# Down projection of a routed feed-forward as three products of rounded pieces, with the pieces streamed from DRAM

## What is computed

```python
xn = _rms_norm(x, scale)
ids = jnp.argmin(_dist2(xn, centroids), axis=-1)
for e in range(8):
    h = jnp.einsum('bsd,dh->bsh', xn, up_w[e])          # 256 -> 2*512
    a, g = jnp.split(h, 2, axis=-1)
    y = jnp.einsum('bsh,hd->bsd', a * silu(g), down_w[e])  # 512 -> 256
    out = jnp.where((ids == e)[..., None], y, out)
x = _layernorm(x + out + skip)
```

## Time and profile before

| | |
|---|---|
| median of 3 runs | 1208.92 us (1208.32 to 1210.83) |
| the profiled execution | 1210.72 us, span from first to last instruction 1209.0 us |
| TensorE / VectorE busy | 92% / 79% of the span |
| ScalarE / GpSimd busy | 55% / 64% |
| mean granted clock | 0.98 |
| data moved | 178.0 MB, 147 GB/s over the span |

### The profile page before, as it was taken

How to read it: one execution, slowest core, us unless ns; L and a number is a source line. 1 busy time by engine, 2 the same in 40 slices (tenths; PEclk the granted TensorE clock), 3 DMA queues, 4 the chain that set the end, 5 groups by cost and what they waited for, 6 DMA issues and landing times.

```text
span 1209.0 us, 27857 instructions
## 1 busy us (share of the span) xinstructions
PE 1114.7 (92%) x8283; PEld 831.4 (69%) x8315; DVE 957.7 (79%) x2437; ACT 667.6 (55%) x1417; POOL 771.6 (64%) x933
## 2 busy tenths in 40 slices
PE   4899998999999999999999999889999999999996
PEld 3766665666666666666666666668788888888885
DVE  7558998999999999999999998978755555555553
ACT  4266775777777776777777777663222222222221
POOL 4736888888998998998889884246433333333333
PEclk9989998999999999999999999979999999999998
DMA  5767777665665656656655645113554444454442
GB/s 127 188 166 203 179 193 173 199 161 148 153 152 153 154 138 155 159 150 152 158 136 157 149 118 132 39 30 103 174 159 137 148 153 154 153 153 146 147 153 88
DMA packets 124097, 178.04 MB, mean 147 GB/s; under 512 B 13670, under 2 KB 111599, under 8 KB 117776
## 3 DMA queue, kind: packets, MB, share of 16 engines
q1 hardware_dynamic: 117456, 159.65, 50.2%
q0 software_dynamic: 6528, 16.99, 4.7%
HBM read 124.47 MB, written 53.03 MB: 147 GB/s over the span
## 4 chain that ended last, share of the span: by engine, by line
PE 39%; DVE 36%; issue 10%; POOL 7%; DMA 4%; SPq 2%; ACT 1%; POOLq 0%; DVEq 0%; ACTq 0%
DVE neg_max_sb L1556 14%; PE Y L488 10%; PE G L450 8%; PE A L450 8%; DVE oq L1755 4%; DVE u L1574 4%; POOL buckets L849 3%; PE GT L460 2%; POOL state L805 2%; PE M L1186 2%; PE S L1229 2%; DMA neg_max<-nm_row 2%; DVE stx L1540 2%; PE O L1178 2%; DVE st L1540 1%
## 5 line engine op out<-in xcount | busy, mean ns | idle before, releaser
L1556 DVE TENSOR_REDUCE neg_max_sb<-S 128x2 f32<-128x512 f32 x512 | 327.5, 681 | 41.4 <-PE S L1229 40.8
L1019 ACT ACTIVATE probs<-T 128x512 f32<-128x512 f32 x512 | 277.7, 595 | 138.2 <-PE T L1242 123.8
L1229 PE MATMUL S<-k_st,q_st 48*128 48x256 f32 x1024 | 208.3, 312 | 33.0 <-DVE neg_max_sb L1556 30.9
L1229 PEld LDWEIGHTS S<-k_st,q_st 48*128 48x128 f32 x1024 | 141.3, 185 | 104.5 <-issue 71.5
L1242 PE MATMUL T<-q_st,k_st 49*128 49x256 f32 x1024 | 206.2, 313 | 6.8 <-ACT probs L1019 3.0
L1242 PEld LDWEIGHTS T<-q_st,k_st 49*128 49x128 f32 x1024 | 142.2, 187 | 22.0 <-ACT probs L1019 14.6
L428 ACT ACTIVATE gT<-GT 128x512 f32<-128x512 f32 x71 | 42.4, 598 | 207.1 <-PE GT L460 203.7
L1178 PE MATMUL O<-probs,v_aug 128*32 128x256 f32 x2048 | 141.4, 395 | 0.8 <-ACT probs L1019 0.7
L408 POOL DMA_INDIRECT out<-res,token x71 | 76.0, 1070 | 102.1 <-DVE res L575 97.0
L488 PE MATMUL Y<-dn_sb,gT 128*128 128x256 f32 x568 | 134.5, 379 | 2.4 <-DMA dn_sb<-in_L_ffn_down_w 1.7
L849 POOL DMA_INDIRECT buckets<-row,slot x64 | 68.9, 1077 | 82.9 <-DVE slot L1810 71.9
(11 more groups left out here) (210 smaller groups left out, 2599.0 us busy)
## 6 DMA issues: line engine op xcount, KB each, us to landing
dn_sb<-in_L_ffn_down_w SPq DMA_DIRECT2D x71, 512.0 KB
k_st<-k_pieces SPq DMA_DIRECT2D x64, 256.0 KB, 3.8
q_st<-q_pieces SPq DMA_DIRECT2D x64, 256.0 KB, 3.6
xr<-buckets SPq DMA_DIRECT2D x71, 129.0 KB
xt<-in_x SPq DMA_DIRECT2D x32, 256.0 KB, 6.2
ct<-in_ctx SPq DMA_DIRECT2D x32, 256.0 KB, 6.9
k_pieces<-k_hi SPq DMA_DIRECT2D x32, 256.0 KB, 3.6
k_pieces<-k_lo SPq DMA_DIRECT2D x32, 256.0 KB, 3.7
```

Of the source, the lines that this page charges most:

```text
L1019: a_.activation(probs[:, h % 8].rearrange("p k t -> p (k t)"), T_ps[h % 2][:, :], ACT.Exp, scale=DH ** -0.5).then_inc(s["exp_ok"], 1)
L1229: last = t_.matmul(S_ps[h % 2][:, c * TOK:(c + 1) * TOK], q_st[h // HPC][base:base + STACK, h % HPC, c * P:(c + 1) * P], k_st[h // HPC][ba ...
L1556: v.tensor_reduce(neg_max[:, cur.mod(2), :, h], S_ps[h % 2][:, :].rearrange("p (c t) -> p c t", c=NTC), AX.X, ALU.max, negate=True).then_i ...
```

## The change

The down projection is done as the up projection is: three float32r products (hi x hi, hi x lo, lo x hi) in place of one float32 product. For that `down_w` is cut once. Ahead of the attention steps SyncE loads all 4 MB of it into the still empty `up_sb`; in step 0 ScalarE rounds the 8 experts (`upper_down`), in steps 0 and 1 VectorE subtracts (`lower_down`), and in steps 1 to 8 SyncE stores both pieces of one expert each (2 x 512 KB) into the new DRAM tensor `down_pieces`. `UP_STEPS` moves to steps 9 to 16. In phase two a tile's `load_down` brings both pieces, 1 MB in rows of 8 KB, where it was 512 KB in rows of 1 KB. `gT` becomes a rounded piece from ScalarE, with a single buffer, and a rest from VectorE, and Y waits for the rest. `gated` takes the place of `gate` in SBUF, and some small tensors of phase two move.

```diff
@@ constants
-UP_STEPS = (0, 1, 2, 3, 4, 5, 6, 7)
+DOWN_STEPS = (1, 2, 3, 4, 5, 6, 7, 8)
+UP_STEPS = (9, 10, 11, 12, 13, 14, 15, 16)
+DOWN_HI_AT = {(0, h): (h // 2,) for h in range(0, H, 2)}
+DOWN_LO_AT = {(0, 5): (0,), (0, 8): (1,), (0, 11): (2,), (0, 14): (3,), (1, 2): (4,), (1, 6): (5,), (1, 10): (6,), (1, 14): (7,)}
@@ build()
+        down_dram = nc.dram_tensor("down_pieces", (E, P, 2 * DNW), F32)
@@ experts()
-            gT = sb2("gT", [P, 2, HCH * P])
-            dn_sb = sb2("dn_sb", [P, 2, DNW])
+            gated = gate
+            gT = sb2("gT", [P, 2, HCH * P], F32R)
+            dn_sb = sb2("dn_sb", [P, 2, 2, DNW], F32R)
...
-            dn_v = down_w.rearrange("e (o p) n -> p (e o) n", p=P)
+            dn_v = down_dram.rearrange("e p n -> p e n")
@@ experts(), load_down(d) on SyncE
-                    sp.dma_start(dn_sb[:, d.mod(2)].rearrange("p (o n) -> p o n", o=HCH), dn_v[:, bass.ds(r, HCH), :]).then_inc(dn_in[d.mod(2)], 16)
+                    sp.dma_start(dn_sb[:, d.mod(2)].bitcast(F32).rearrange("p (a w) n -> p a (w n)", a=1), dn_v[:, bass.ds(r, 1), :])\
+                        .then_inc(dn_in[d.mod(2)], 16)
@@ experts(), ScalarE
-                        wait(act, "y_pe", m - 2)
-                        a_.activation(gT[:, m.mod(2)], GT_ps[:, :], ACT.Copy).then_inc(z["gT_ok"], 1)
+                        wait(act, "y_pe", m - 1)
+                        a_.activation(gT[:, 0], GT_ps[:, :], ACT.Copy).then_inc(z["gT_ok"], 1)
@@ experts(), TensorE
-                        wait(pe, "gT_ok", m - 1)
+                        wait(pe, "gT_lo", m - 1)
...
-                        wait(pe, "gT_ok", m)
+                        wait(pe, "gT_lo", m)
                         wait(pe, "y2_ok", m - 1)
-                        for c in range(HCH):
-                            last = t_.matmul(Y_ps[:, 0:C], gT[:, m.mod(2), c * P:(c + 1) * P], dn_sb[:, m.mod(2), c * C:(c + 1) * C],
-                                             start=(c == 0), stop=(c == HCH - 1))
+                        terms = [(w, d, c) for c in range(HCH) for w, d in ((0, 0), (0, 1), (1, 0))]
+                        for k, (w, d, c) in enumerate(terms):
+                            last = t_.matmul(Y_ps[:, 0:C], gT[:, w, c * P:(c + 1) * P], dn_sb[:, m.mod(2), d, c * C:(c + 1) * C],
+                                             start=(k == 0), stop=(k == len(terms) - 1))
@@ experts(), VectorE, between `res` of f and `xsT` low of n
+                    if active(m):
+                        wait(dve, "gT_ok", m)
+                        v.tensor_tensor(gT[:, 1], GT_ps[:, :], gT[:, 0].bitcast(F32), ALU.subtract).then_inc(z["gT_lo"], 1)
@@ SyncE, ahead of the attention steps
+                for e in range(E):
+                    dst = up_sb[:, e * DNW:(e + 1) * DNW].bitcast(F32).rearrange("p (o n) -> p o n", o=HCH)
+                    sp.dma_start(dst, down_w[e].rearrange("(o p) n -> p o n", p=P)).then_inc(s["down_in"], 16)
@@ SyncE, attention steps
+                def store_down(e):
+                    sp.wait_ge(s["down_lo"], e + 1)
+                    for w in range(2):
+                        at = slice(((1 - w) * E + e) * DNW, ((1 - w) * E + e + 1) * DNW)
+                        sp.dma_start(down_dram[e, :, w * DNW:(w + 1) * DNW], up_sb[:, at].bitcast(F32)).then_inc(s["down_out"], 16)
                 def ups(e):
+                    if e == 0:
+                        sp.wait_ge(s["down_out"], 2 * 16 * E)
...
+                    if t.k in DOWN_STEPS:
+                        store_down(DOWN_STEPS.index(t.k))
                     if t.k in UP_STEPS:
                         ups(UP_STEPS.index(t.k))
@@ ScalarE, attention steps (called from DOWN_HI_AT)
+                def upper_down(e):
+                    if e == 0:
+                        act.wait_ge(s["down_in"], 16 * E)
+                    a_.activation(up_sb[:, (E + e) * DNW:(E + e + 1) * DNW], up_sb[:, e * DNW:(e + 1) * DNW].bitcast(F32), ACT.Copy)\
+                        .then_inc(s["down_hi"], 1)
@@ VectorE, attention steps (called from DOWN_LO_AT)
+                def lower_down(e):
+                    dve.wait_ge(s["down_hi"], e + 1)
+                    at, hi = slice(e * DNW, (e + 1) * DNW), slice((E + e) * DNW, (E + e + 1) * DNW)
+                    v.tensor_tensor(up_sb[:, at], up_sb[:, at].bitcast(F32), up_sb[:, hi].bitcast(F32), ALU.subtract).then_inc(s["down_lo"], 1)
```

More of the change, by code:

```diff
@@ L307, in experts, with sb_small @@
-            rs3 = sb2("rs3", [P, 2])
-            token = sb2("token", [P, 2], U32)
+            small = [0]
+            def sb_small(name, shape, dt=F32):
+                n = 1
+                for d in shape[1:]:
+                    n *= d
+                small[0] += (n + 7) // 8 * 8
+                return sb2(name, [P] + shape[1:], dt)[0:shape[0]]
+            count = sb_small("count", [1, E])
+            tiles, ends = scan[:, 0, E:2 * E], scan[:, 1, E:2 * E]
+            full = sb_small("full", [1, E])
```

49 lines of the change are left out of this document (26 added, 23 removed).

## The result

The changed kernel took 1232.9 us, median of four runs (1221.7 to 1238.1). The kernel before took 1209.9 (1208.3 to 1214.1) beside it. The ratio is 1.019, 95% interval 1.0147 to 1.0234: slower, by 18 to 28 us. The forecast was 1225 with a range of 1206 to 1254, so direction and range held; the sum was 8 us short, and two of its terms were mis-sized in opposite directions. The profiled execution is the slowest of the four (1238.1, span 1236.3, mean granted clock 0.974) and its span lies 27 us above the one before, of which phase one is 13 and phase two 14.

What follows compares the result with a forecast made beforehand. It took mostly VectorE's maxima to bound phase one and TensorE's Y, G and A phase two. Start 1, pieces 3, loaded steps 11, tile loop -3 and first tiles 4 made +16 on 1208.92: 1225 us, range 1206 to 1254.

Steps and rivals of the forecast that it cites:

- The mechanism of the wait: Phase two tile loop: Y waits for VectorE's subtraction, queued behind `res`, from +2.80 to +3.49 after Y's end.
- Its size: Phase two tile loop with the wait: period 5.14 against 5.18, -0.04 x 57 = -3 us (-9 to 0).
- The first tiles: Start of phase two: longer waits for down weights and added subtractions, less the shorter Y, +4 us (0 to 8).
- The transfer: Phase two: a tile's 1 MB lands in 5.2 us, with 5.4 us of room, and counts as hidden.
- rival 1: Phase two: down-weight loads pace the tiles, landing 6.05, period 5.48, +17 instead of -3, 1245 us; chance 0.24.
- Rival 3: Phase two: the new weight loads are not hidden, Y takes 2.64, period 6.3, about 1305 us; chance 0.04.
- Start and pieces: Phase one: 4.2 MB loaded ahead, +1 us (0 to 5); rounding and subtracting the pieces, +3 us (0 to 10).
- Eight more loaded steps: Phase one: eight more steps carry a 1 MB transfer, 1.47 us each; +11 us taken, from 0 to 26.
- the tiles' +1: Phase two altogether: -3 for the steady tile loop and +4 for the first tiles, +1 us.

Runs made afterwards that it cites:

- the tiles alone: Phase one of the kernel before with the change's phase two, each tile loading 1 MB of other weights: 1226.4 us, ratio 1.0103.
- the subtraction first: Changed kernel with VectorE's subtraction for gT moved ahead of its wait for the root: 1229.6 us, ratio 1.0139.
- half the bytes: Changed kernel with subtraction and TensorE's register read moved earlier, loading only the rounded down piece, 512 KB a tile: 1205.2 us, ratio 0.9969.
- the earlier issue: Changed kernel with subtraction and TensorE's read moved earlier, plus SyncE's reads ahead of its waits and pieces issued right behind the rows: 1209.8 us, ratio 0.9948.
- the read ahead of GT: Changed kernel with the subtraction ahead of the root wait and TensorE's register read ahead of the wait for `gated`: 1221.7 us, ratio 1.0068.
- without the stores: Change's phase one with pieces made but not stored, up weights in steps 9 to 16, phase two of before: 1215.4 us, ratio 1.0024.
- 0 (loads): Kernel before with 8 MB of up weights loaded a second time in steps 9 to 16: 1213.6 us, ratio 1.0001.
- +6.3 (stores): Kernel before with eight times 2 x 512 KB stored from `up_sb` in steps 9 to 16: 1214.2 us, ratio 1.0052.
- the whole phase one: Phase one of the change, pieces made and stored but unread, with phase two of the kernel before: 1223.8 us, ratio 1.0096.

## Why the prediction was right, and where it was not

**The mechanism of the wait: right.** The subtraction behind `res` was put at +2.80 to +3.49 from Y's end; it was at +2.80 to +3.48. TensorE's work shrinks to 4.89, and this loop took its place.

**Its size: wrong by 0.12, which turned the sign of the term.** From the subtraction's end to Y's end the forecast had 0.05 for the signal, 0.22 for the first load and 12 x 0.115 = 1.38. Measured: 0.11 to Y's first product, and a Y of 1.66, which is 1.43 unwaited and 0.23 more. So the first load was right, Y was 0.05 longer (12 x 0.119), and the signal 0.06. The loop became 5.25 rather than 5.14, and that of 5.18 before lies between. Of the other 0.05 of the mean, 0.02 is the one late transfer, and the rest are two tiles in every eight of the runtime loop that take 5.34 to 5.38. Instead of -0.04 x 57 = -3 the term was +0.115 x 57 = +7. A term that is the difference of two nearly equal loops has no safe sign; its range of -9 to 0 had to reach above zero.

**The first tiles: right in size.** +4 was forecast. From SyncE's first issue of down pieces to the thirteenth, before took 84.2 us (813.23 to 897.47) and after 89.1 (825.89 to 915.01): +4.9. With the +7 this is nearly all of the +12.5 of the tiles alone. The forecast put 2 of its 4 down to the subtraction. The runs point at the transfer for nearly all of it: with the subtraction first the same stretch still takes 89.1, with half the bytes 84.8, and with the earlier issue 84.3.

**The transfer: right for the change.** The landing was 5.16 where 5.2 was forecast (in the read ahead of GT, where the chain shows it), and while it ran the rate in the window below (columns as above) was 442 GB/s, more than the 389 of the 1 KB rows. Among windows of 1 us over the tiles from 930 to 1190 the busiest has 475 GB/s, and 400 in the kernel before (all transfers together; windows this short are rough, some have a DMA share above 1). Row length and size of the transfer both changed, so this doesn't part them.

```profile
987.00:987.50 0.50, 0.50 (x6) 0.50 (x5) 0.38 (x1) 0.00 (x0) 0.00 (x0) 1.00 1.09 442
```

The Trainium skill, "DMA: Bandwidth & Descriptors", section "Bandwidth", has 6.15 us and 341 GB/s for 1 MB issued from GpSimd. The trace differs: SyncE's 1 MB landed in 5.16, issue included, and its rate in the busiest windows is above 341. "Hidden" was right for 50 of 51 tiles, since the wait for the subtraction covers it. So rival 1 wasn't the bound of the change, although its sign of a period over 5.25 appeared. It is the bound behind the wait and the register read: with both gone, the period is 5.18 by the transfer.

**Rival 3: fell.** Loads of 128x128 hide behind products of 256 columns, 0.118 apart. The rule of the Trainium skill, "TensorE: Matmul & The Clock Gate", section "The mechanism", that a load overlaps a running product only when the row groups differ, would have given Y 2.64; Y took 1.43. Another sentence of that section, by which a load is also pulled ahead when it goes to the background weight buffer, fits the trace.

**Start and pieces: right in sum.** +1 and +3 forecast, +2.9 (-1 to +7) measured without the stores. The change's trace puts +3.8 at the start, where +1 was forecast, and +3.6 in the two steps, of which some 2.2 are the pieces' at an equal clock. VectorE's subtractions took 1.2 to 3.3, at most 0.1 over the bound of 3.2, by the line's own row (min/median/max ns, first and last start):

```profile
L1702 DVE TENSOR_TENSOR up_sb<-up_sb x8: 1209/1292/3328, 53.7 to 93.7; 128x1024 fp32r<-128x1024 f32 x8
```

**Eight more loaded steps: mechanism seen, size too large.** The forecast took 1.47 a step from five steps against five others of one execution. Where the same steps are compared with and without a load, the excess over before is 0.8 to 0.9, 6 to 7.5 us in all. By time the eight more transfers are worth 0 (loads), +6.3 (stores), and +8.7 (the whole phase one less the variant without stores). One of them reads 0 where its own trace reads 6; the ten steps that nothing touches differ by 2.9, so these don't contradict each other, but they don't settle it to better than some 4 us either. The trip through DRAM is as long as supposed in the loaded steps, and it moves with the loads: in steps 9 to 16 of the change the long one takes 6.5 to 9.0 from issue to issue, this being the longest, and without stores the same trips of steps 1 to 8 fall to 3.4 to 5.1. What of it reaches the time is the 0.8 or so a step.

```profile
305.74 8.97 DMA neg_max<-nm_row
```

So the term of +11 was about +7, the tiles' +1 was +12, and the total of +16 became +23.

## What to carry to other kernels

Before shortening a step of a bound engine, lay out the loops under it with the same care as the sum: here four lay within 0.4 us (5.25 the wait, 5.14 a register read, some 5.1 a transfer, 4.89 the engine's work), and the change paid only once all three had been moved. Where a trace names what ended a wait, look whether the wait would have been shorter without it: 13 of 14 waits put down to the transfer ended with the subtraction. Where a wait on another engine is added, put its work ahead of whatever that engine itself waits for, and take register reads and transfers' issues ahead of the waits. An excess per step is measured by moving the cause to other steps, not by comparing two stretches of one execution.

## What was not expected of the hardware

- A register read from SBUF on TensorE's queue, between two groups of matmuls, cost 0.25 us of its time in each tile and let the next load start 1.07 us behind the end of the operation that both waited for; ahead of the wait it cost nothing (G 1.39).
- With 1 MB issued from a second queue, ahead of 129 KB of the first, the small transfer took 2.27 to 5.00 us, and the kernel 3.7% more than the same kernel with one queue and the small transfer first.
- Four transfers of 256 KB cost more than one of 1 MB at the end of the step: +14.5 us over eight steps, over half of it as TensorE's busy time at a lower granted clock.
- Twelve 128x128 weight loads in a row stood 0.118 us apart behind float32r products of 256 columns.
- With 1 MB a tile in rows of 8 KB the DMA engines moved 475 GB/s in their busiest microsecond, with 512 KB in rows of 1 KB 400.
